# The last stage of a two-layer transformer with a routed mixture of experts: one long piece of answers per partition, a buffer for each chunk, and one chunk added up beside the expert units

## What is computed

```
scores = softmax(xf @ w_router);  expert_weights, top_experts = top_k(scores, 2)
...                                   # a stable sort by expert; offsets within the expert
valid = offsets < capacity            # capacity 1024; slot = expert * capacity + offset
h = gelu(einsum('ech,ehf->ecf', xb, w1))
y = einsum('ecf,efh->ech', h, w2).reshape(E * capacity, hs)
out = zeros((T, hs)).at[src].add(flat_w[order][:, None] * yv)   # yv: y where valid, else 0
ffn = out + bias
x = x + gb * ffn                      # gb: one row of 128 per sequence
```

## Time and profile before

| What | Value |
|---|---|
| Median of three runs | 1026.92 us (1026.81 to 1027.49) |
| The profiled execution, whole | 1026.7 us |
| Its span, first to last instruction | 1025.0 us |
| PE busy | 927.5 us, 90% of the span |
| DVE busy | 621.7 us, 61% |
| ACT busy | 564.7 us, 55% |
| POOL busy | 282.1 us, 28% |
| TensorE clock granted, mean | 0.959 |
| Mean rate of the transfers | 65 GB/s |

### The profile page before, as it was taken

The page is one execution under the profiler, slowest core; times in us unless marked ns, Lnnn a source line. Parts: engine busy times, 40 slices in busy tenths (PEclk is TensorE's granted clock), DMA queues, the critical chain, the costliest instruction groups (busy, mean ns, idle before and its releaser), DMA issues.

```text
span 1025.0 us, 20305 instructions
## 1 busy us (share of the span) xinstructions
PE 927.5 (90%) x7910; PEld 761.2 (74%) x7910; DVE 621.7 (61%) x1968; ACT 564.7 (55%) x951; POOL 282.1 (28%) x357
## 2 busy tenths in 40 slices
PE   3679998989989999999999999999999996999960
PEld 2445554555679898988989888898898885889960
DVE  7787787787469685454654636555455855852226
ACT  2287778786776555445455546546445563654420
POOL 6946154120201111023203232022322003077660
PEclk9688999989999999999999999999999998999995
DMA  5433443434771000000000000000000013023218
GB/s 157 123 126 113 151 145 99 135 118 162 193 172 65 1 1 2 1 1 19 3 2 21 1 22 1 6 18 1 22 1 17 6 42 103 14 73 94 77 35 248
DMA packets 85243, 66.39 MB, mean 65 GB/s; under 512 B 8098, under 2 KB 75672, under 8 KB 85148
## 3 DMA queue, kind: packets, MB, share of 16 engines
q1 hardware_dynamic: 80724, 56.80, 18.8%
q0 software_dynamic: 4352, 8.28, 2.5%
q10 hardware_dynamic: 72, 0.02, 0.0%
HBM read 33.76 MB, written 31.59 MB: 64 GB/s over the span
## 4 chain that ended last, share of the span: by engine, by line
PE 74%; ACT 10%; DVE 6%; DMA 3%; SPq 3%; issue 3%; POOL 1%; POOLq 0%; ACTq 0%; DVEq 0%
PE psum L1414 25%; PE psum L1391 19%; PE psum L1236 4%; PE psum L1174 3%; PE psum L1466 2%; PE psum L1190 2%; PE psum L1217 1%; PE psum L1144 1%; PE psum L1295 1%; ACT big L2317 1%; PE psum L1338 1%; PE psum L1316 1%; ACT ew L2212 1%; PE psum L1166 1%; PE psum L1250 1%
## 5 line engine op out<-in xcount | busy, mean ns | idle before, releaser
L1414 PEld LDWEIGHTS psum<-ew,big 128*128 128x128 f32 x2560 | 315.7, 191 | 18.7 <-ACT big L2317 3.3
L1414 PE MATMUL psum<-ew,big 128*128 128x128 f32 x2560 | 322.2, 276 | 1.2 <-ACT big L2317 1.0
L2317 ACT ACTIVATE big<-psum,cols 128x512 f32<-128x512 f32 x256 | 174.3, 689 | 174.3 <-PE psum L1391 173.9
L1391 PE MATMUL psum<-parts,q_stack 128*128 128x512 f32 x640 | 219.1, 423 | 2.0 <-ACT big L2324 1.4
L1757 DVE TENSOR_REDUCE maxes<-psum 128x4 f32<-128x1024 f32 (+1 forms) x96 | 113.8, 1217 | 26.1 <-PE psum L1190 25.8
L1391 PE MATMUL psum<-parts,k_stack 128*128 128x512 f32 x320 | 125.9, 393 | 0.0
L2584 POOL DMA_INDIRECT routed<-big,slot_i x64 | 62.8, 981 | 225.3 <-DVE slot_i L2072 180.0
L1883 DVE SCALAR_TENSOR_TENSOR hT<-psum,gates,hT 128x128 f32<-128x128 f32 x256 | 71.8, 344 | 84.8 <-PE psum L1414 84.5
L1391 PEld LDWEIGHTS psum<-parts,q_stack 128*128 128x128 f32 x640 | 106.1, 190 | 13.3 <-ACT big L2324 1.9
L2594 POOL DMA_INDIRECT answers<-hT,to x64 | 62.2, 973 | 69.1 <-DVE hT L2091 50.8
L1391 PEld LDWEIGHTS psum<-parts,k_stack 128*128 128x128 f32 x320 | 60.1, 188 | 13.6
(11 more groups left out here) (381 smaller groups left out, 1535.9 us busy)
## 6 DMA issues: line engine op xcount, KB each, us to landing
q_stack<-q_pieces SPq DMA_DIRECT2D x32, 192.0 KB
k_stack<-k_pieces SPq DMA_DIRECT2D x32, 192.0 KB
routed<-empty_row SPq DMA_DIRECT2D x4, 1040.0 KB, 12.0
big<-routed SPq DMA_DIRECT2D x16, 260.0 KB, 2.9
answers<-gb_tok SPq DMA_DIRECT2D x4, 1024.0 KB, 10.7
q_pieces<-gb_tok SPq DMA_DIRECT2D x16, 192.0 KB, 2.1
k_pieces<-gb_tok SPq DMA_DIRECT2D x16, 192.0 KB, 2.1
x<-in_L_attn_x SPq DMA_DIRECT2D x4, 512.0 KB, 6.3
```

Source lines behind the costliest of these rows:

```text
L1391: last = eng.matmul(bank(i), w1_part(wp, e)[:, fs], parts[2 * xk + xp][:, :], start=n == 0, stop=n == 2)
L1414: last = eng.matmul(psum[:, i, k * C:(k + 1) * C], hid[:, r, f, k * P:(k + 1) * P], ew2[:, e, f, :], start=f == 0, stop=f == FC - 1)
L2317: eng.activation(hid[:, held("hid", "up", n, e, f), f, :], bank(held("bank", "up", n, e, f)), ACT.Relu, bias=col("L0_ffn_b1", e * FC + f)) ...
```

## The change

Three things change.

1. **Layout of `answers`.** The row of a token is now found by chunk, then partition, then choice, then block: the eight rows (two choices, four blocks) that one partition needs for one chunk lie in one piece of 4 KB. `yin` becomes one transfer of 512 KB instead of two of 256 KB. The table of destinations (`iota`) is computed in the new order, with one instruction as before. The scatter of `send` and the zeros are the same instructions.
2. **A buffer for each chunk.** `yb` has eight entries: two in the upper half of `hT`, two in `big1` behind the fetch rings, four in `tmp`. No `yin` waits for a `sum`. Each `yin` waits for all `bias` steps, after which these places are free.
3. **Chunk 0 early.** `yin` of chunk 0 waits only for the sends of units 0 to 7. Its `sum` is planned with less urgency. A function that would let POOL add chunks (`add`) is written too, but the list `BY_POOL` is empty, so it is never called.

```diff
-YR = 4
+BY_POOL = ()
...
     for n in range(NCH):
-        p.step("yin", n, work="sp:1.2 dma:5", after=[("send", u) for u in range(UNITS)] + ([("sum", n - YR)] if n >= YR else []))
-        p.step("sum", n, work="dve:2.15", after=[("yin", n), *[("bias", b) for b in range(B)]])
-        p.step("store", n, work="sp:.42 dma:2.5", after=[("sum", n)])
+        p.step("yin", n, work="sp:.6 dma:3.5", after=[("send", u) for u in range(UNITS if n else EARLY)] + [("bias", b) for b in range(B)])
+        added = p.step(adds(n), n, work="pool:4.5" if n in BY_POOL else "dve:2.15", urgent=0 if n else -20, after=[("yin", n)])
+        p.step("store", n, work="sp:.42 dma:2.5", after=[added])
...
-        y_in = [semaphore(f"y_in{i}") for i in range(YR)]
+        y_in = [semaphore(f"y_in{i}") for i in range(NCH)]
...
-        ans_v = answers.rearrange("(k n p) c -> k p n c", k=TOPK, p=P)
-        yb = [t[:, h * 2 * CHUNK:(h + 1) * 2 * CHUNK].rearrange("p (k t c) -> p k t c", k=TOPK, c=C)
-              for t in (big1, hT) for h in range(YR // 2)]
+        ans_v = answers.rearrange("(n p k t) c -> n p k t c", p=P, k=TOPK, t=CT)
+        LEFT = 2 * CHUNK
+        XB = RINGS * CT * ROW
+        yb = [r.rearrange("p (k t c) -> p k t c", k=TOPK, c=C) for r in (
+            *(hT[:, RINGS * CHUNK + h * LEFT:RINGS * CHUNK + (h + 1) * LEFT] for h in range(2)),
+            *(big1[:, XB + h * LEFT:XB + (h + 1) * LEFT] for h in range(2)),
+            *(tmp[:, 2 * h:2 * h + 2, :].rearrange("p a n -> p (a n)") for h in range(4)))]
...
             def yin(n):
-                r = n % YR
                 for k in range(RINGS):
-                    w.wait_ge(answer_out[k], 16 * CT * UNITS // RINGS)
-                if n >= YR:
-                    w.wait_ge(*done("sum", n - YR))
-                for k in range(TOPK):
-                    eng.dma_start(yb[r][:, k, :, :], ans_v[k, :, CT * n:CT * (n + 1), :]).then_inc(y_in[r], 16)
+                    w.wait_ge(answer_out[k], 16 * CT * (UNITS if n else EARLY) // RINGS)
+                for b in range(B):
+                    w.wait_ge(*done("bias", b))
+                eng.dma_start(yb[n].rearrange("p k t c -> p (k t c)"),
+                              ans_v[n].rearrange("p k t c -> p (k t c)")).then_inc(y_in[n], 16)
...
             def sum_(n):
-                ts, both = slice(CT * n, CT * (n + 1)), yb[n % YR][:, 0, :, :]
-                w.wait_ge(y_in[n % YR], 16 * TOPK * (n // YR + 1))
-                eng.tensor_tensor(both, both, yb[n % YR][:, 1, :, :], ALU.add).then_inc(chain.sem, chain.more())
+                ts, both = slice(CT * n, CT * (n + 1)), yb[n][:, 0, :, :]
+                w.wait_ge(y_in[n], 16)
+                eng.tensor_tensor(both, both, yb[n][:, 1, :, :], ALU.add).then_inc(chain.sem, chain.more())
...
-                eng.iota(slot_i[:, :, :], pattern=[[TOK, TOPK], [P, NT]], base=0,
-                         channel_multiplier=1).then_inc(chain.sem, chain.more())
+                eng.iota(slot_i[:, :, :].rearrange("p k (n t) -> p k n t", t=CT), pattern=[[CT, TOPK], [P * TOPK * CT, NCH], [1, CT]],
+                         base=0, channel_multiplier=TOPK * CT).then_inc(chain.sem, chain.more())
```

More of the change, by code:

```diff
@@ L71, with adds @@
 FIRST = ((0, 4), (4, 8), (8, 16), (16, 24), (24, 32))
+def adds(n):
+    return "add" if n in BY_POOL else "sum"
 def first_group(b):
@@ L122 @@
     "bias": ("bias", "dve"),
-    "yin": ("final", ""), "sum": ("final", "dve"), "store": ("final", ""), "wmod1": ("setup", ""), "free": ("fill", ""),
+    "yin": ("final", ""), "sum": ("final", "dve"), "add": ("final", "pool"), "store": ("final", ""), "wmod1": ("setup", ""), "free": ("fill", ""),
 }
@@ L1071, in yin @@
             def yin(n):
-                r = n % YR
                 for k in range(RINGS):
-                    w.wait_ge(answer_out[k], 16 * CT * UNITS // RINGS)
-                if n >= YR:
-                    w.wait_ge(*done("sum", n - YR))
-                for k in range(TOPK):
-                    eng.dma_start(yb[r][:, k, :, :], ans_v[k, :, CT * n:CT * (n + 1), :]).then_inc(y_in[r], 16)
+                    w.wait_ge(answer_out[k], 16 * CT * (UNITS if n else EARLY) // RINGS)
[3 more added lines that the diff above has]
+                              ans_v[n].rearrange("p k t c -> p (k t c)")).then_inc(y_in[n], 16)
             def store(n):
                 ts = slice(CT * n, CT * (n + 1))
-                w.wait_ge(*done("sum", n))
+                w.wait_ge(*done(adds(n), n))
                 eng.dma_start(out_v[:, ts, :], x[:, ts, :]).then_inc(result_out, 16)
@@ L2597, in send, with add @@
                         oob_is_err=False).then_inc(answer_out[k], 16)
+            def add(n):
+                ts, both = slice(CT * n, CT * (n + 1)), yb[n][:, 0, :, :]
+                w.wait_ge(y_in[n], 16)
+                eng.tensor_tensor(both, both, yb[n][:, 1, :, :], ALU.add).then_inc(chain.sem, chain.more())
+                for k in range(B // 4):
+                    w.wait_ge(*done("sg_m", 1, k))
+                w.wait_ge(chain.sem, chain.n)
+                eng.tensor_tensor(both.rearrange("p (b t) c -> p b t c", t=TPB),
+                                  both.rearrange("p (b t) c -> p b t c", t=TPB),
+                                  gb_tok[:, BPC * n:BPC * (n + 1), :].unsqueeze(2).to_broadcast([P, BPC, TPB, C]),
+                                  ALU.mult).then_inc(chain.sem, chain.more())
+                for b in range(BPC * n, BPC * n + BPC):
+                    w.wait_ge(*done("bias", b))
+                w.wait_ge(chain.sem, chain.n)
+                eng.tensor_tensor(x[:, ts, :], x[:, ts, :], both, ALU.add).then_inc(sem("add"), 1)
             mine = {"masks": masks, "late": late, "ln_p": ln_p, "rest": rest, "cut": cut, "gv_a": gv_a, "gv_w": gv_w, "gv_v": gv_v, "am_s": am_s, "blk": blk, "gam": gam_, "tab": tab,
-                    "la_g": la_g, "rt_d": rt_d, "send": send}
+                    "la_g": la_g, "rt_d": rt_d, "send": send, "add": add}
             for step in p.orders["pool"]:
```

## The result

| What | Before | After |
|---|---|---|
| Median, 22 runs of each in alternation | 1028.42 us (1024.36 to 1031.06) | 1025.45 us (1021.96 to 1028.23) |
| Ratio after to before | | 0.9973, 95% interval 0.9963 to 0.9983 |
| The profiled execution, whole | 1026.7 us | 1022.55 us |
| Its span | 1025.0 us | 1020.8 us |
| Last scatter landed | 1000.76 | 999.62 |

The kernel became 0.27% faster. The forecast was 1024.1 us against 1026.92, which is the same ratio, 0.9973. The times themselves fit less well. The median of 1025.45 lies in the range of 1023.1 to 1025.6, near its upper end, but above the 1024.87 at which the prediction would have called the kernel faster. So the gain came out as forecast, and the level and the spread of single executions did not.

What follows compares the result with a forecast made beforehand. DVE was taken to set the end, with the DMA engines close behind. One chunk fewer and a quicker first read took 2.8 us off the span (1025.0 to 1022.2), so the median went from 1026.92 to 1024.1 us; range 1023.1 to 1025.6.

Steps and rivals of the forecast that it cites:

- What bounds the kernel: At the end, DVE's read-sum-store work on the chunks sets the time, 2.06 us a chunk, with the DMA engines close behind.
- the sum of the end: Seven sums from 1004.5 finish on DVE at 1019.4, with 2.77 us behind them: span 1022.2 against 1025.0.
- T: Stretch from the last scatter's landing to the span's end; 24.24 us before, forecast at 21.44.
- the first read: At the start of the end, from SP's issue to DVE's first sum: 3.83 us before, 0.17 us less claimed.
- rival of a quicker first read: One issue and longer pieces save 0.6 us at the start of the end, giving 1023.5 us; chance 0.10.
- Chunk 0 beside the units: Reading and adding chunk 0 after unit 9's answers costs nothing there; its data land about 4.2 us after issue.
- cover: Slack of 4.5 us between the delayed remainder of unit 12, ending at 957.3, and PE's first use at 961.81.
- The flow: At the end, reads flow at 315 GB/s, stay ahead of DVE, and stores behind them cost nothing.
- the queue of stores: Rival: mixed reads and stores at the end flow at only 270 GB/s, giving 1025.1 us; chance 0.14.
- slow long pieces: Rival: 4 KB pieces flow slower than 512-byte ones, so the last read bounds; about 1033 us at 157 GB/s; chance 0.07.
- The buffers: With a buffer for each chunk, SP issues seven reads in a row and DVE's 0.35 us wait for a read goes.
- the last step: From span 1022.2 to median 1024.1 us, using a profiled execution 1.7 us above its span and 0.2 below the median.

Runs made afterwards that it cites:

- e6_light_new: Changed kernel with one DVE instruction per chunk instead of three (second answer and gate left out), all reads and stores kept; T 18.15 us.
- e3_four_buffers: Changed kernel with four chunk buffers instead of eight, new layout and early chunk 0 kept; T 21.09 us, ratio to before 0.9970.
- e11_after_again: Changed kernel run again unaltered, in a later series; T 21.18 us, ratio to before 0.9972.
- e5_sum0_plus10: Changed kernel with ten idle DVE instructions added to chunk 0's sum; from unit 9's answers to unit 14's 38.56 us, against 34.36.
- e8_pool_2_5: Changed kernel with chunks 2 and 5 added up by POOL instead of DVE; T 23.36 us, ratio to before 0.9996.
- e10_pe_3_to_7: Changed kernel with PE adding the two answers of chunks 3 to 7, DVE doing the other two instructions; T 22.79 us, ratio to before 0.9976.
- e7_light_old: Changed kernel with one DVE instruction per chunk and the old answers layout in 512-byte pieces; T 19.18 us.

## Why the prediction came out as it did

**What bounds the kernel, and the sum of the end: right.** The seven sums stand at 2.06 and 2.15 us, DVE's stretch is 14.87 us against a forecast 14.9, and 2.72 us come behind it against 2.77. T was forecast at 21.44 us (1022.2 - 1000.76) and is 21.18. The largest part of the difference is the first read: 3.59 us where 3.74 was expected, and 3.91 before. I had taken 0.17 us of a possible 0.6, and it was 0.32, about half way to the rival of a quicker first read. The Trainium skill ("SBUF — State Buffer", section "The DMA setup-cost knee") has a fixed 2 us and the bytes over 436 GB/s, from which an estimated 3.2 us follow. The transfer itself lies in the chain with 3.50 us, so the rule is close but too low here.

**Chunk 0 beside the units: right in its cost, and its cover confirmed.** The yin went out at 949.11 and its data let the sum begin at 953.65, 4.5 us later; 4.2 had been estimated. Hence a wait of 0.34 us that was not foreseen, inside the cover. The runs with 4 and 10 added instructions bracket that cover between 2.9 us and 7.2. The stand puts it at 4.8 for the ten (7.23 - 2.40), of which 0.38 is the wait for data that was absent there, so near the 4.5 that the prediction read.

**The flow: the mechanism right, the size cautious.** DVE waits for no read, and the stores find a queue only at first: landing takes 2.3 us at least, 3.4 in the median and 7.2 at most. The first reads flow at 344 to 414 GB/s, not 315. This removes the two rivals that live on it, the queue of stores and slow long pieces, and e6_light_new shows 3.0 us of room.

**The buffers: right by their little weight.** The wait of 0.35 us did go, but the four buffers of e3_four_buffers would have done as well. The prediction credited the buffers with it; with long pieces and four buffers it is gone too.

**The step that failed: what one execution is worth.** It is the last step, from the span to the time and its range: "the profiled execution took 1.7 us more than its span and was 0.2 below the median, so the median goes from 1026.92". The prediction took three runs within 0.7 us (1026.81 to 1027.49) for the spread and the one profiled execution for the level. The range allowed 0.2 us for the scatter, 0.3 for small gaps and what the rivals cost; a difference between executions of the same kernel ahead of the end was put at nothing, without a reason. The runs showed in its place that executions of one kernel lie over 6 us: 1024.36 to 1031.06 before and 1021.96 to 1028.23 after. For the profiled execution the span was forecast at 1022.2 us and was 1020.8. Of these 1.4 us 0.26 are T, and 1.14 are the last scatter, which landed at 999.62 and not at the expected 1000.8. For the median the forecast was 1.35 us too low, and the median of before was itself 1.5 us higher in the 22 runs than in the first three. The ratio was forecast well. That it was exact to four digits is luck in part: its interval is 0.9963 to 0.9983.

The same spread is in the two profiled executions. The answers of unit 9 were done 1.12 us earlier in the trace after (952.18 against 953.30), although the only part of the change ahead of them is where the answers are written. The lead is there where the expert units begin, before anything is scattered to `answers` (from 893.10 on). The same products, first of the kernel before, then after:

```profile
869.38 2.05 PE L1439 MATMUL psum<-ident,tmp 128*128 128x128 f32 x16 [1.42 <-ACT tmp L2331]
```

```profile
868.26 2.05 PE L1449 MATMUL psum<-ident,tmp 128*128 128x128 f32 x16 [1.62 <-ACT tmp L2341]
```

Stretches of 5 us up to them, first of the kernel before, then after (columns as above, the clock third from the end):

```profile
860.00:865.00 5.00, 4.39 (x12) 3.15 (x13) 1.62 (x5) 1.43 (x3) 0.00 (x0) 0.50 0.79 215
865.00:870.00 5.00, 3.58 (x19) 2.92 (x18) 3.56 (x9) 3.63 (x8) 0.00 (x0) 0.83 0.00 0
```

```profile
860.00:865.00 5.00, 4.41 (x14) 3.21 (x15) 1.66 (x6) 1.45 (x3) 0.00 (x0) 0.59 0.80 214
865.00:870.00 5.00, 3.38 (x27) 3.02 (x26) 4.52 (x13) 4.16 (x10) 0.00 (x0) 1.00 0.00 0
```

PE had stood idle for some 7 us before this point in both. In the execution after, the clock was back at 2.4 GHz a little earlier: (0.59 - 0.50) x 5 + (1.00 - 0.83) x 5 = 1.3 us of full clock more, about the 1.12 gained. Among the 22 runs of the changed kernel the time goes with the granted clock in the same way: 1021.96 us at 0.962 and 1028.23 at 0.955, with a correlation of -0.69. Its square is 0.48, so the mean clock goes with about half of the variance. That the clock makes a part of the spread is therefore likely, but how much was not set by an experiment, and e11_after_again shows that an execution can be longer at the full clock too. Part of the lead of the profiled span, 1.14 of 4.2 us, isn't the change's.

## What to carry to other kernels

Where an engine works without a break up to the end, one piece of its work moved beside an earlier stage is worth its period (2.05 us here, of 2.06), and the cover has to be read at the first instruction that uses what is pushed back, not from busy shares. Faster transfers or more buffers in front of such an engine are worth the first read and its few waits, and one of the two can be enough. Before work is given to another engine, look at what the two share and at the clock that an idle TensorE will start with. A range for one time must come from many executions of the same kernel; three that agree say little, and the ratio in alternating runs is steadier than either time.

## What the runs showed of the hardware that I had not expected

- Behind a stand of PE of 2.40 us the granted clock was 0.50 for about 3 us (e5_sum0_plus10), so that 4.2 us were lost in all.
- DVE and POOL, each with 128x512 float32 instructions on two on-chip inputs, took turns: 0.69 us of DVE became 1.59 to 1.75, each ending 0.54 to 0.56 us behind POOL's instruction (e8_pool_2_5).
- Adding two 128x512 float32 tiles by products with the identity shows as four matmuls: 3.42 us at 1.2 GHz and 1.72 at 2.4 GHz (e10_pe_3_to_7).
- The first reads in pieces of 4 KB flowed at 344 to 414 GB/s and in pieces of 512 bytes at 273 to 315, at nearly the same share of the DMA engines; with more reads in flight pieces of 512 bytes reached 346 (e7_light_old).
